# Windowed attention with an expert layer on 8 cores: the scatter of the attention weights is issued one step later, and their use one step earlier

## What is computed

```python
q = _ln(silu(x @ Wq).reshape(B, L, H, D), q_g, q_b)          # H=16, D=64
kv = silu(x @ Wkv)
k = _ln(kv[..., :C].reshape(B, L, H, D), k_g, k_b).reshape(B, L, C)
v = kv[..., C:]
wp = silu(x @ Wwin + bwin)
...
scores = jnp.stack([jnp.einsum('blhd,blhd->blh', q, k_pad[:, w:w + L].reshape(B, L, H, D)) for w in range(K)], axis=-1) * SCALE
soft_mask = jax.nn.sigmoid((width[..., None] - rel) * sharp[..., None])
attn = jax.nn.softmax(scores - (1.0 - soft_mask) * MASK_PENALTY, axis=-1)
out = sum((attn[..., w][..., None] * v_pad[:, w:w + L].reshape(B, L, H, D) for w in range(K)))
return silu(out.reshape(B, L, C) @ Wout)
```

## Time and profile before

| | us |
|---|---|
| two timed runs | 2322.29 and 2495.70, median 2408.99 |
| profiled execution | 2314.07 |
| its span, slowest core (core 4) | 2312.5 |
| spans of the eight cores | 2285.5 to 2312.5 |
| mean granted TensorE clock of the cores | 0.772 to 0.777 |
| busy: TensorE, weight loads, ScalarE, VectorE, GpSimd | 1533.4, 787.9, 563.9, 542.5, 117.5 |

### The profile page before, as it was taken

The page is one execution under the profiler, slowest core; times in us unless marked ns, Lnnn a source line. Parts: engine busy times, 40 slices in busy tenths (PEclk is TensorE's granted clock), DMA queues, the critical chain, the costliest instruction groups (busy, mean ns, idle before and its releaser), DMA issues.

```text
span 2312.5 us, 22763 instructions; the slowest of 8 cores (2285.5 to 2312.5 us)
## 1 busy us (share of the span) xinstructions
PE 1533.4 (66%) x8376; PEld 787.9 (34%) x8492; DVE 542.5 (23%) x814; ACT 563.9 (24%) x836; POOL 117.5 (5%) x136
## 2 busy tenths in 40 slices
PE   0594144458467989889807922444675779889995
PEld 0242122324433434444304411223334334344442
DVE  0164221101311221222212443111023122212223
ACT  0353122224321112021204521222243202021122
POOL 0120000000200000000001100000002000000000
PEclk9997555556588999999957955555575989999998
DMA  9222212220182525520292222212103625534203
GB/s 220 53 38 37 71 47 56 56 45 1 19 127 37 73 41 79 85 52 1 38 227 32 37 59 50 68 35 69 32 1 57 89 37 76 80 64 73 37 1 109
DMA packets 142341, 139.37 MB, mean 60 GB/s; under 512 B 73239, under 2 KB 106136, under 8 KB 142234
## 3 DMA queue, kind: packets, MB, share of 16 engines
q0 software_dynamic: 60960, 84.55, 23.6%
q1 hardware_dynamic: 76890, 36.60, 6.3%
q10 hardware_dynamic: 4384, 16.78, 2.2%
HBM read 189.36 MB, written 33.10 MB: 96 GB/s over the span
## 4 chain that ended last, share of the span: by engine, by line
PE 60%; DMA 18%; DVE 7%; ACT 6%; issue 5%; another core or an unknown queue 2%; SPq 0%; DVEq 0%; ACTq 0%; POOL 0%; POOLq 0%
PE ps_A L336 37%; PE ps_B L336 14%; PE ps_t L342 9%; DVE bscr L364 3%; DMA scdram<-swide 3%; DMA wpool<-Su 3%; ACT R L355 2%; DMA wpool<-Wd 2%; DMA qpark<-Wd 2%; DMA kpark<-awdram 2%; DMA wrf<-Wr 1%; DMA bscr<-x 1%; DMA wpool<-Sd 1%; DVE xtm L364 1%
## 5 line engine op out<-in xcount | busy, mean ns | idle before, releaser
L336 PE MATMUL ps_A<-wpool,R 128*128 128x512 bf16 x2118 | 499.1, 387 | 37.8 <-DMA wpool<-Su 17.6
L342 PE MATMUL ps_t<-sb_ident,bscr 128*128 128x128 bf16 x1312 | 147.0, 264 | 361.5 <-DVE bscr L364 230.6
L355 ACT COPY R<-ps_t 128x512 bf16<-128x512 bf16 (+2 forms) x242 | 186.4, 784 | 775.8 <-PE ps_t L342 775.6
L336 PEld LDWEIGHTS ps_A<-wpool,R 128*128 128x128 bf16 x2176 | 211.3, 99 | 282.1 <-issue 55.4
L336 PE MATMUL ps_B<-wpool,R 128*128 128x512 bf16 (+1 forms) x1072 | 237.4, 367 | 42.6 <-DMA wpool<-Sd 25.4
L342 PEld LDWEIGHTS ps_t<-sb_ident,bscr 128*128 128x128 bf16 x1312 | 112.8, 118 | 414.4 <-issue 382.0
L351 ACT ACTIVATE fscr<-ps_A 128x512 f32<-128x512 f32 x236 | 140.7, 599 | 436.7 <-PE ps_A L336 425.6
L336 PE MATMUL ps_A<-qpark,R 128*128 128x512 bf16 x750 | 177.3, 380 | 3.9 <-DVE xtm L364 2.9
L336 PEld LDWEIGHTS ps_B<-wpool,R 128*128 128x128 bf16 x1088 | 101.1, 100 | 167.1 <-issue 58.0
L336 PE MATMUL ps_A<-R 128*128 128x64 bf16 (+1 forms) x512 | 86.5, 228 | 57.6 <-ACT R L355 57.6
L342 PE MATMUL ps_t<-sb_ident,R 128*128 128x128 bf16 (+1 forms) x384 | 74.5, 289 | 64.3 <-DMA R<-awdram 57.3
(11 more groups left out here) (133 smaller groups left out, 1345.7 us busy)
## 6 DMA issues: line engine op xcount, KB each, us to landing
scdram<-swide SPq DMA_DIRECT2D x16, 648.0 KB, 3.0
xtm<-x ACTq DMA_DIRECT2D x2, 4096.0 KB, 29.7
wpool<-Wkv POOLq DMA_DIRECT2D x4, 2048.0 KB, 36.1
qpark<-Wg POOLq DMA_DIRECT2D x8, 1024.0 KB, 28.8
kpark<-Wu POOLq DMA_DIRECT2D x8, 1024.0 KB, 33.8
wpool<-Wg POOLq DMA_DIRECT2D x8, 1024.0 KB, 16.1
wpool<-Wu POOLq DMA_DIRECT2D x8, 1024.0 KB, 20.9
qpark<-Wd POOLq DMA_DIRECT2D x8, 1024.0 KB, 9.9
```

The costliest lines, as they stand in the source:

```text
L336: e.matmul(d, l, r, start=s0, stop=s1),
L342: P.op("tensor", lambda e, d=dst, s=src: e.transpose(d, s, ident[:]), rd=[src, ident[:]], wr=[dst], tag=tag, strips=strips)
L355: P.op("scalar", lambda e, o=out, i=in_: e.copy(o, i), rd=[in_], wr=[out], tag=tag)
```

## The change

The scatter is taken out of `emit_A` and becomes a function of its own, `emit_scatter`. Step i now issues, behind the two score writes, first the scatter of tile i - 1, then `emit_B(i - 2)` with its read-back, then `emit_A(i)` with its gather. Behind the loop stand the scatter of tile 7 and the two emit_B of tiles 6 and 7.

```diff
                 vop("tensor_tensor",
                     abfc[i % 2][:].rearrange("p (h w) -> p h w", h=NH),
                     [lg3, rib], (ALU.mult,), tag=f"anrm{hx}")
+
+            def emit_scatter(i):
                 dma("sync",
                     bass.AP(aw_dram[i].tensor, 0,
                             [[2305, 128], [144, NH], [1, K17]]),
@@
                     swide[:, 1296:2304], tag=f"scoutB{hx}")
-                if i >= 3:
-                    emit_B(i - 3)
+                if i >= 1:
+                    emit_scatter(i - 1)
+                if i >= 2:
+                    emit_B(i - 2)
                 emit_A(i)
-            emit_B(NT - 3)
+            emit_scatter(NT - 1)
             emit_B(NT - 2)
             emit_B(NT - 1)
```

## The result

The changed kernel is slower by 1.2%: the ratio to the kernel before is 1.0117, with a 95% interval of 1.0089 to 1.0146 (medians 2346.3 us of 11 runs and 2321.04 us of 10 runs, 25 us apart). The profiled execution took 2346.0 us, its spans are 2319.1 to 2344.4 us. The forecast was 2361.7 us, 2.1% slower; the range of 2322 to 2410 holds the time.

What follows compares the result with a forecast made beforehand. The attention stretches were taken as a chain of waits through read-back and emit_B, no engine full. From 2314.1 us, -5.4 - 3 + 54 + 4 - 2 = +47.6 gave 2361.7 us, range 2322 to 2410.

Steps and rivals of the forecast that it cites:

- step 1, the gather: Attention step 1: its gather, on the chain, now comes behind tile 0's scatter; 2 us each, +4 for both halves.
- step 2, the moved emit_B and one read-back: Step 2 of each half gains an emit_B, +31.4 together, plus one read-back delayed by 4.5 us each.
- steps 3 to 6, 8 read-backs: In these attention steps the read-back TensorE waits for lands 4.5 us later behind the scatter; +36.
- step 7, read-back less the wait removed: Loop's last step: read-back 4.5 us later per half; SyncE's wait before the scatter gone, about -3 us together.
- behind the loop: After each half's loop: one emit_B fewer, -36.8 together; the first read-back has less traffic beside it, -2.
- the rest of the kernel: Everything outside the two attentions: the sum held no term for it, 0.
- the wait removed: SyncE's wait for normalized weights before the scatter: worth 0, except in step 7, about -3 us for both halves.
- The first rival: In the steps, the scatter costs only its queue place, 12 x 1.4 to 12 x 3, +10 to +30; chance 0.22.
- the third: Rival: the read-back is served beside the scatter, delay near 0, moved emit_B decides; -10.4, 2304 us; chance 0.08.
- D: Added delay of a step's read-back issued behind the scatter: 4.5 us, 12 times, +54 (16.8 to 86.4).
- The signs: Expected in the trace: steps' read-backs 7 to 10 us, steps with an emit_B 42 to 46, step 1 25 to 28.
- the main case: D from 3 to 6 us in the steps, 2344 to 2380 us; chance 0.56.

Runs made afterwards that it cites:

- experiment 1: Kernel before with emit_B(i - 2) in place of emit_B(i - 3), scatter left in emit_A; ratio to kernel before 0.996, median 2314.16 us.
- experiment 2: Changed kernel with emit_B(i - 3) and three emit_B behind the loop, so only the scatter is moved; ratio 1.015 to kernel before.
- experiment 8: Kernel before reordered: read-back of tile i - 2, emit_A(i) with its scatter, then emit_B(i - 2)'s computing; ratio 0.9675, median 2246.11 us.
- experiment 3: Changed kernel with the scatter issued behind emit_A(i)'s gather instead of ahead of the read-back; ratio 0.985 to kernel before.
- experiment 7: Changed kernel with the scatter issued on SyncE between the two score writes, some 3 us sooner; ratio 1.0173 to kernel before.
- experiment 6: Changed kernel with the scatter on ScalarE's queue, held until the A score write has landed; ratio 1.0003 to kernel before.
- experiment 5: Changed kernel with the scatter on ScalarE's queue, where it went out before the score writes; ratio 0.9945, median 2296.13 us.
- experiment 4: Changed kernel with a dense 68 KB write, 128 runs of 544 bytes, in the scatter's place; ratio 0.9889, median 2286.35 us.
- experiment 10: Kernel of experiment 8 with read-back and emit_B one tile sooner, and one score write in place of two; ratio 0.9588, median 2227.14 us.

## Why the forecast was right and wrong

The sum of the prediction against the trace, both halves together, from the mean step times of the eight cores:

| term, us | forecast | measured |
|---|---|---|
| step 1, the gather | +4 | +3.6 |
| step 2, the moved emit_B and one read-back | +31.4 + 9 = +40.4 | +38.6 |
| steps 3 to 6, 8 read-backs | +36 | +32.5 |
| step 7, read-back less the wait removed | +9 - 3 = +6 | +4.8 |
| behind the loop | -36.8 - 2 = -38.8 | -41.8 |
| both attentions | +47.6 | +37.8 |
| the rest of the kernel | 0 | -8.4 |

**Right.** What bounds the steps: the read-back's landing and emit_B (experiments 1, 2 and 8). That the wait removed was worth nothing outside step 7. That the scatter ahead of the read-back is what costs, on each of 12 steps, and not the earlier use (1 against 2). The value of the moved emit_B: experiment 1 alone gains 0.4%, some 9 us against the 5.4 forecast. The first rival (only the scatter's 1.4 us) and the third (the read-back passes beside it) are out by the landings: D is 4.0, the median read-back of a step 8.4 us in 96 of them against 4.4 in 80 before. The time alone would not have told: +25 us lies in the first rival's +10 to +30. The signs came as written: read-backs of 7.7 to 9.3 us, steps with an emit_B of 44 to 45 us in the mean, step 1 of 26.4 and 27.5.

**Wrong, first: the size of D, and with it the end of the loop.** The 12 x 4.5 = +54 should have been 12 x 4.0 = +48. The step that failed was "I stay nearer to the smaller value but above it, because half 0 has shown double: D = 4.5". The 11.54 us of half 0 are no property of a scatter with a read-back behind it: experiment 2 has two read-backs right behind the last scatter, in the same order as before, and the first lands after 7.4 to 8.1 us on all cores. That is no more than the 8.4 us of a step, where there is only one, so the second read-back, which I gave as the other reason, does not add to the landing. What half 0 of the kernel before had besides was the two cores of each pair at the same place, 1 to 2 us apart (last section; not shown to be the cause). Half 1, 4.5 to 6.6 us apart, gave 7.91 and D = 3.7, the nearer row. That it is so near to 4.0 is in part luck: at that place of the changed kernel the read-back lands after 7.2 us, not after the 8.4 of a step. The 0.5 us too much counts 12 times, 6 us, and the end of the loop gave 3 us more than forecast, since its first read-back now lands after 6.9 to 7.6 us in both halves.

**Wrong, second: a term that the sum does not have.** It put the rest of the kernel at nothing, because the engines' programs there are unchanged. But 8.4 us net came back in it (9.3 behind the attentions, 0.9 lost ahead of them; 4.2 net against the second profile of before). The chain of core 4 before and after, two waits for the expert weights of half 0:

```profile
625.68 30.68 DMA wpool<-Su
...
721.41 15.58 DMA wpool<-Sd
```

```profile
639.58 24.39 DMA wpool<-Su
...
728.97 13.24 DMA wpool<-Sd
```

The same loads are waited for less. Why stays open; the last section has what goes with it. The forecast of +47.6 us and the +29.3 of the mean spans are 18 us apart: 8.4 by this term, some 6 by D, 3 by the end of the loop. With D at 4.0 and nothing else changed the sum would have given 2355.7 us; that the 2346.3 measured still lies inside the main case (2344 to 2380), at its edge, owes to its width.

The chance for slower by over 2% (0.44) was too high by that; within 2% (0.55) was the case that came.

## What to carry to other kernels

Before a small-run scatter is moved off a wait, look at what the queue has behind it at its new place: here the wait was covered, and the new place was on the chain. A delay read from one row is to be read from every core and every half first, since the same two DMAs in the two halves of one program differed by 3.6 us, for a reason that their order does not give. And where a chain passes through one engine's program order, try the order before the transfers: exchanging the softmax and emit_B took 2.9% off the kernel (experiment 8 against 1), nearly the 3.3% that lie between the best and the worst place of the scatter (3 and 7).

## What the runs showed of the hardware

**A scatter of small runs delays the transfers around it, whatever their queue.** By the time from the scatter's issue to the read-back's (experiment's number in brackets): a read-back issued 2.8 us ahead of it, 4.4 us to landing (experiment 3); read-back 0.5 us after the scatter, 8.4 us in one queue and 7.9 to 8.1 from another (6); 3.4 us after it, 6.3 us (7, half 1); 5 us after it, 4.3 us in half 1 and 4.8 in half 0 (5). The same bytes in runs of 544: 4.5 us (4). These are medians; single ones in one queue run from 7.7 to 9.3. The landings stand in order: in the changed kernel the scatter at 1536.04 + 7.3 = 1543.3 and the read-back at 1536.56 + 8.2 = 1544.8; in experiment 7 the scatter at 1501.9, the B write at 1502.6, the read-back at 1504.0. The Trainium skill, "DMA: Bandwidth & Descriptors", section "Queues, rings and completion order", has it that a semaphore increment lands only after every earlier write of that DMA engine, across its queues. Within one queue these landings agree. From two queues they come the other way round: in experiment 6 the read-back landed at 1541.4 and the scatter, issued first, at 1541.7; in experiment 5 the A write, issued 0.3 us behind the scatter, landed at 1537.0 and the scatter at 1538.1.

That order is not what makes the read-back late. The DMA view has the bytes under way, here in steps of 0.25 us: the changed kernel from 1536 to 1546 (core 0), then the kernel before from 1574 to 1584 (core 4).

```profile
GB/s 0 226 419 371 258 258 403 150 52 51 51 51 51 2 37 166 18 92 203 74 74 92 111 92 111 92 129 92 111 297 257 244 184 140 128 90 67 18 0 0
```

```profile
GB/s 0 0 0 0 452 435 371 419 242 182 295 166 350 479 369 332 278 110 101 130 125 115 27 2 0 0 0 0 0 0 0 0 0 0 0 0 0 0 0 0
```

In the first the B score write comes first, then the scatter at some 51 GB/s for 1.4 us, then the read-back at mostly 75 to 200 for 4.9 us, to 1544.4. In the second the read-back has mostly 166 to 479 GB/s and is through in 2.1 us, by 1578.5. The packets of the read-backs in all steps say the same (medians, kernel before and changed kernel): first packet 1.8 and 3.0 us after the issue, first to last packet 2.3 and 5.0 us, last packet to landing 0.36 and 0.39 us. So of the 4.0 us 1.2 is the wait behind the scatter's packets, which is the prediction's lower end for D, and 2.7 is that the read-back's own packets come slower while the scatter, whose last packet left 4.0 us before its landing, is not yet finished. Nothing is left for a finished read-back that waits for the scatter's completion. Why the packets come slower is not shown.

**The two cores of a pair (0 and 1, 2 and 3, and so on) wait longer for DMAs where they stand at the same place of the program.** The distance of a pair is taken here from each core's own first instruction; that the two start at the same moment is assumed, no row shows it. One execution shows the relation well: experiment 7, half 0, where cores 0 and 1 leave the attention 9.6 us apart, and cores 4 and 5 0.3 us. The first read-back behind the loop in the chain of core 0 and of core 5:

```profile
510.86 7.88 DMA R<-awdram
```

```profile
555.13 12.31 DMA R<-awdram
```

All of cores 0 to 3 (pairs 9.6 and 7.0 us apart) have 7.2 to 7.9 us there, all of 4 to 7 (0.3 and 0.8 us apart) 11.5 to 12.7; their steps take 41 to 44 and 45 to 48 us, and the same cores 4 and 5, 9.7 us apart in half 1, take 42 as well. The granted clock is 0.50 on core 0 and on core 5 in that stretch, so it is not the clock. It holds for the weight loads too. In the 12 profiles of this study (all but that of experiment 6), 23 pairs leave the first attention under 4 us apart, and the waits for expert weights on their chains up to the second attention sum to 86.3 us in the mean; the 23 pairs that are 7 us and more apart have 78.0, with the stretch 825.5 and 816.0 us long. It is so within one execution too: in experiment 10 two pairs are 17 us apart and have 77 us, two are 0.8 and 0.9 us apart and have 90 and 91. This goes with what came back in the changed kernel (pairs 8.2 to 11.9 us apart) and in experiment 3 (11.1 to 11.9), and did not in the kernel before and in experiment 1 (0.7 to 2.6). In 12 executions of the kernel before (those beside experiment 1) the spans of a pair's cores differ by 9.7 us in the mean, in 11 of the changed kernel by 16.5. That two cores share the bandwidth of their memory is in the Trainium skill ("HBM Reference", section "Specifications (TRN2)"), which fits; that the loss goes with the distance at which they run the same program is what these rows add. The distance differs by kernel, so an edit may change it in a stretch far away. What in the kernel sets it was not found, and no experiment changed the distance alone: that the distance is the cause and not a sign of it is not shown.
